# A fused attention and feed-forward kernel: the scores' maximum and bias moved ahead of the probabilities' low halves in VectorE's step

## The chip, the cores and the metric

One core of a Trainium2 chip (trn2). The metric is the device time of one execution of the whole kernel, in microseconds (us). The kernel before has a median of 798.86 us over three runs (798.53, 798.86 and 799.95).

## The reference

The input x is 16 batches of 128 rows by 256. Four blocks follow, each added to x: a first attention over the context with 8 heads of 16, a feed-forward block with ternary weights, a second attention, and a gated ternary feed-forward block. The change is in the second attention only. For it the reference computes, per batch:

```
q = rope(rms_norm(y @ Wq.T))            16 heads of 128,  y = layernorm(x)
k = rope(rms_norm([ctx; y] @ Wk.T))      4 heads of 128,  256 keys
v = [ctx; y] @ Wv.T
probs = softmax(q k.T / sqrt(128))      4 query heads share one key head
x = x + (probs v) @ Wo.T
```

## The kernel before

The second attention is `part_c`. Its work is cut into 64 units: 16 batches times 4 groups, one group being one key head with its four query heads. It is a software pipeline written out by hand: every engine runs a loop over steps s, and in step s each stage works on the unit u = s minus that stage's lag. The lags are PROJ 4 (projections, norm, rope), QK_TURN 5 (a DMA transposes queries and keys), SCORE 6, PROBS 7, LOWS 8 (a DMA transposes the low halves), ATTEND 9, OUT 10. Once per batch, in every fourth step, come HALVES (lag 2), ROWS (lag 1, the layernorm's rows) and LAST (lag 14, the residual). Nothing reorders the work: each engine executes its list in order, and a wait on a semaphore holds everything behind it on that engine.

Precision is kept by splitting float32 values into a float16 high half and a float16 low half. A product takes three passes (high by high, high by low, low by high; `PASSES`), so each stage has an instruction for the high half and one for the low half.

In one step of the steady state the engines do this, in this order (lines of the kernel before):

- **VectorE**: the share of the probabilities, as a scaling (L1321) and a reciprocal (L1324); L1321 waits for ScalarE's four exponentials of the previous step. Then queries times cosine and sine (L1330). Then the low half of the attended rows (L1338). Then `lows(probs, 0)`, two instructions of L1311: the low halves of the probabilities of heads 0 and 1. Once per batch the residual, x_rows (L1345). Then the maximum over the scores of a unit (L1351), which waits for TensorE's scores, and the bias made of it (L1355). Then `lows(probs, 1)`, two more of L1311. Then keys times cosine and sine (two of L1366, which wait for the norm factor r that ScalarE makes at L1301) and the low half of v (L1370). Once per batch the statistics of new rows (L1376, L1380), and a step later their normalised rows (L1385).
- **ScalarE**: the high half of the attended rows (L1245), the high halves of the probabilities (four of L1252, which wait for the share), the sums of squares (four of L1266 after L1330, two of L1272), the high half of v (L1276), a logarithm (L1280), once per batch two small ones (L1286, L1289), then the first exponential (L1235), which waits for the bias, the factor r (L1301) and three more exponentials.
- **TensorE**: the query projection (six matmuls, L1406), the key and value projection (twelve, L1417), the scores (twelve, L1431), the attended rows (six, L1444), the output projection (twelve, L1459). L1417 waits for VectorE's L1370 of the previous step, since there is one bank for keys and values. L1444 waits for L1338. L1459 of a batch's first group waits for the residual L1345 of the batch before it, since there is one bank for the output; by the lags both stand in the same step (s - 10 and s - 14).
- **GpSimd**: the rotation of queries (L1189), their high half (L1193), their low half (L1220, which waits for this step's bias), and the keys' (L1223 to L1228, from L1366 on). The SyncE queue issues the transposes (L1138 for probabilities, L1153 for queries and keys, L1159 for rows).

The stages before and behind overlap with it. The first feed-forward block's last batches share its first steps, the second feed-forward block's first batches its last ones, on the same engines.

The waits that the steps of the prediction use:

```
eng.wait_ge(S["scores"], u + 1)          # VectorE, before L1351
wait(eng, S["v_lo"], u)                  # TensorE, before L1417
if g == 0:
    wait(eng, S["out"], b)               # TensorE, before L1459
eng.wait_ge(S["exps"], u + 1)            # VectorE, before L1321
```

Of the kernel before, what the change touches and what calls it, by code (L numbers as in the profile page):

```python
# [21 lines left out]
ALU = mybir.AluOpType  # L22
# [15 lines left out]
def wait(eng, sem, value):  # L38

    if value > 0:  # L40
        eng.wait_ge(sem, value)
# [847 lines left out]
W_SCALE = 64.0  # L889
# [164 lines left out]
def part_c(core):  # L1054


    c = core
    GROUPS = KV_HEADS
# [8 lines left out]
    LAST = OUT + GROUPS  # L1067
    STEPS = TOTAL + OUT + 1
    P_SCALE = 1024.0
    A_SCALE = 2.0**-10  # L1070
# [34 lines left out]
    A_BANK, O_BANK = c.bank(0), c.bank(1)[:, 0:D]  # L1105
# [10 lines left out]
    S = {n: c.sem("c_" + n) for n in (  # L1116
        "eps", "stats", "rstd", "y", "y_hi", "y_lo", "tables", "q", "kv", "ss_k", "ss_q", "r", "q_cs", "q_rot", "k_cs",
        "k_rot", "v_hi", "v_lo", "q_hi", "q_lo", "k_hi", "k_lo", "scores", "top", "bias", "exps", "share", "p_hi",
        "p_lo", "attn", "a_hi", "a_lo", "o", "out")}
# [5 lines left out]
    def unit(s, lag):  # L1125

        u = s - lag
        return u if 0 <= u < TOTAL else None

    def batch(s, lag):  # L1130


        u = s - lag
        return u // GROUPS if 0 <= u < TOTAL and u % GROUPS == 0 else None
# [172 lines left out]
    def vector(eng):  # L1307
        def lows(u, half):
            eng.wait_ge(S["p_hi"], 2 * u + half + 1)
            for h in range(2 * half, 2 * half + 2):  # L1310
                last = eng.scalar_tensor_tensor(p_hl[:, u % 2, 1, h, :], s_banks(u)[:, h, :],  # L1311
                                                share[:, u % 2, h:h + 1], p_hl[:, u % 2, 0, h, :],
                                                ALU.mult, ALU.subtract)
            last.then_inc(S["p_lo"], 1)

        for s in range(STEPS + 1):
            probs, proj, score, attend = unit(s, PROBS), unit(s, PROJ), unit(s, SCORE), unit(s, OUT)
            if probs is not None:
                u = probs
                eng.wait_ge(S["exps"], u + 1)  # L1320
                eng.tensor_scalar(part[:, u % 2, :], total[:, u % 2, :], 1.0 / P_SCALE, None, ALU.mult)\  # L1321
                   .then_inc(S["share"], 1)
                eng.wait_ge(S["share"], 2 * u + 1)
                eng.reciprocal(share[:, u % 2, :], part[:, u % 2, :]).then_inc(S["share"], 1)  # L1324
            if proj is not None:
                u, b = proj, proj // GROUPS
                eng.wait_ge(S["tables"], b + 1)
                eng.wait_ge(S["q"], u + 1)
                wait(eng, S["q_rot"], u)
                eng.tensor_tensor(  # L1330
                    q_cs[:, :, :, :],
                    Q_BANK.rearrange("p (h d) -> p h d", h=SHARE).unsqueeze(1).broadcast_to([P, 2, SHARE, HEAD_DIM]),
                    turn["q"][:, b % 2, :, :].unsqueeze(2).broadcast_to([P, 2, SHARE, HEAD_DIM]), ALU.mult)\
                   .then_inc(S["q_cs"], 1)
            if attend is not None:
                u = attend
                eng.wait_ge(S["a_hi"], u + 1)
                eng.scalar_tensor_tensor(a_t[:, u % 2, 1, :], A_BANK, A_SCALE, a_t[:, u % 2, 0, :], ALU.mult,  # L1338
                                         ALU.subtract).then_inc(S["a_lo"], 1)
            if probs is not None:  # L1340
                lows(probs, 0)
            b = batch(s, LAST)
            if b is not None:
                eng.wait_ge(S["o"], GROUPS * (b + 1))
                eng.scalar_tensor_tensor(c.x_rows[:, b, :], O_BANK, 1.0 / (W_SCALE * W_SCALE * P_SCALE * A_SCALE),  # L1345
                                         c.x_rows[:, b, :], ALU.mult, ALU.add).then_inc(S["out"], 1)
            if score is not None:
                u = score
                eng.wait_ge(S["scores"], u + 1)
                wait(eng, S["bias"], u - 1)  # L1350
                eng.tensor_reduce(top[:, u % 2, :], s_banks(u), AX.X, ALU.max).then_inc(S["top"], 1)  # L1351
                eng.wait_ge(S["top"], u + 1)
                eng.wait_ge(S["r"], 2 * (u + 1))
                wait(eng, S["exps"], u - 1)
                eng.scalar_tensor_tensor(bias[:, u % 2, :], top[:, u % 2, :], -1.0, r_q(u), ALU.mult, ALU.mult)\  # L1355
                   .then_inc(S["bias"], 1)
            if probs is not None:
                lows(probs, 1)
            if proj is not None:

                u, b = proj, proj // GROUPS
                eng.wait_ge(S["r"], 2 * (u + 1))
                eng.wait_ge(S["v_hi"], u + 1)
                wait(eng, S["k_rot"], u)
                for n in range(2):
                    last = eng.scalar_tensor_tensor(  # L1366
                        k_cs[:, :, n, :], kv_view[:, n, 0, :].unsqueeze(1).broadcast_to([P, 2, HEAD_DIM]), r_k(u, n),
                        turn["k"][:, b % 2, :, n, :], ALU.mult, ALU.mult)
                last.then_inc(S["k_cs"], 1)
                eng.tensor_tensor(v[:, u % V_SLOTS, 1, :, :], kv_view[:, :, 1, :], v[:, u % V_SLOTS, 0, :, :], ALU.subtract)\  # L1370
                   .then_inc(S["v_lo"], 1)
            b = batch(s, 0)
            if b is not None:
                eng.wait_ge(ffn["out"], b + 1)
                wait(eng, S["stats"], 2 * b)
                eng.bn_stats(stats[:, :], c.x_rows[:, b, :]).then_inc(S["stats"], 1)  # L1376
                eng.wait_ge(S["stats"], 2 * b + 1)
                wait(eng, S["y"], b)
                wait(eng, S["rstd"], 2 * b)
                eng.bn_aggr(mv[:, :], stats[:, :]).then_inc(S["stats"], 1)  # L1380
            b = batch(s, ROWS)
            if b is not None:
                eng.wait_ge(S["rstd"], 2 * (b + 1))
                wait(eng, S["y_lo"], b)
                eng.tensor_scalar(y[:, :], c.x_rows[:, b, :], mv[:, 0:1], rstd[:, :], ALU.subtract, ALU.mult)\  # L1385
                   .then_inc(S["y"], 1)
            yield
# [4 lines left out]
    def tensor(eng):  # L1392
        for s in range(STEPS):
# [69 lines left out]
            yield  # L1463

    return sync, pool, scalar, vector, tensor


# [87 lines left out]
```

## Time and profile before

| what | value |
|---|---|
| median of 3 runs | 798.86 us |
| the profiled execution's own time | 800.01 us |
| its span in the trace | 798.3 us |
| granted TensorE clock, mean over the span | 0.961 |
| TensorE matmuls busy | 677.3 us, 85% of the span |
| VectorE busy | 661.1 us, 83% |
| ScalarE busy | 624.3 us, 78% |
| GpSimd busy | 534.5 us, 67% |
| DMA packets | 323795, 99.80 MB |

The second attention takes the larger half of the span: VectorE's first maximum over scores (L1351) starts at 289.4 us and its last at 723.4 us. All four compute engines are in use through it, and in most slices of that stretch TensorE, VectorE and ScalarE each show nine tenths or more.

Engine names in the rows: PE is TensorE's matmul, PEld its weight load, DVE is VectorE, ACT ScalarE, POOL GpSimd, SPq the queue of SyncE. In a timeline a row gives the start in us, the length in us of all the instructions merged into the row, the engine, the line, the operation, what it writes and reads, its shape and how many there are. The bracket at the end is idle time in front of it and who ended it.

### The profile page before, as it was taken

What the parts mean: (1) busy time and instruction counts of PE and PEld (TensorE: products, weight loads), DVE (VectorE), ACT (ScalarE), POOL (GpSimd) and SP (SyncE); (2) the same over time, 40 slices, a digit from 0 to 9 for tenths busy, and PEclk for the clock granted to TensorE, in tenths of its full rate; (3) what the DMA queues carried; (4) which work ended last, traced back from release to release, by engine and by line L of the source; (5) the groups of instructions that cost most, each with busy time, mean ns of one, the idle gap of its engine ahead of it and who ended that gap; (6) DMA issues with size and microseconds to landing.
All of it is one profiled execution on the core that took longest, in us unless ns stands there. A gap on an engine that the chain in (4) does not pass through costs nothing. (4 is left out here: it accounts for less than half of the span.)

```text
span 798.3 us, 17290 instructions
## 1 busy us (share of the span) xinstructions
PE 677.3 (85%) x5139; PEld 423.0 (53%) x5139; DVE 661.1 (83%) x1576; ACT 624.3 (78%) x2122; POOL 534.5 (67%) x764
## 2 busy tenths in 40 slices
PE   0075799999578678999999999999999999978995
PEld 0043255455234345666666666666666666645552
DVE  6756556764689769999999999999999999978994
ACT  0556477777399769999999999999999999968661
POOL 1413756663357888888788878887887888753673
PEclk9997599999799989999999999999999999999997
DMA  8502555542024356897887798788879787865244
GB/s 278 199 1 54 138 155 148 142 129 86 11 67 106 64 106 126 147 144 129 148 139 142 127 154 139 134 138 154 139 135 144 143 136 133 153 113 93 58 125 122
DMA packets 323795, 99.80 MB, mean 125 GB/s; under 512 B 294868, under 2 KB 322934, under 8 KB 323446
## 3 DMA queue, kind: packets, MB, share of 16 engines
q1 hardware_dynamic: 323702, 98.70, 61.7%
q8 instruction: 41, 0.67, 0.4%
q14 instruction: 52, 0.43, 0.2%
HBM read 20.01 MB, written 6.29 MB: 33 GB/s over the span
## 5 line engine op out<-in xcount | busy, mean ns | idle before, releaser
L1235 ACT ACTIVATE psum<-psum,arena 128x256 f32<-128x256 f32 x256 | 135.9, 531 | 21.1 <-DVE arena L1355 21.0
L1311 DVE SCALAR_TENSOR_TENSOR arena<-psum,arena 128x256 f16<-128x256 f32 x256 | 110.9, 474 | 1.1 <-ACT arena L1252 1.1
L1252 ACT ACTIVATE arena<-psum,arena 128x256 f16<-128x256 f32 x256 | 100.3, 474 | 7.4 <-issue 3.4
L1444 PE MATMUL psum<-arena 128*128 128x512 f16 x384 | 94.2, 381 | 8.1 <-DVE arena L1338 7.9
L1189 POOL TENSOR_TENSOR arena<-arena 128x512 f32<-128x512 f32 x64 | 81.1, 1267 | 27.8 <-DVE arena L1330 27.8
L1406 PE MATMUL psum<-wq_t,arena 128*128 128x512 f16 x384 | 94.5, 383 | 5.5 <-ACT arena L1266 2.8
L1431 PE MATMUL psum<-arena 128*128 128x256 f16 x768 | 95.6, 275 | 1.0 <-DMA arena<-arena 0.8
L1459 PE MATMUL psum<-wo_t,arena 128*128 128x256 f16 x768 | 95.0, 274 | 0.1
L305 ACT ACTIVATE arena<-psum 128x1024 f32<-128x1024 f32 x64 | 63.1, 1019 | 33.2 <-PE psum L391 33.2
L1459 PEld LDWEIGHTS psum<-wo_t,arena 128*128 128x128 f16 x768 | 75.5, 98 | 23.2 <-issue 1.1
L1220 POOL TENSOR_TENSOR arena<-arena 128x512 f16<-128x512 f32 x64 | 74.1, 1157 | 20.0 <-DVE arena L1355 19.9
L1431 PEld LDWEIGHTS psum<-arena 128*128 128x128 f16 x768 | 75.3, 99 | 11.4 <-DMA arena<-arena 1.6
L1351 DVE TENSOR_REDUCE arena<-psum 128x4 f32<-128x1024 f32 x64 | 77.8, 1215 | 2.7 <-PE psum L1431 2.4
L1330 DVE TENSOR_TENSOR arena<-psum,arena 128x1024 f32<-128x1024 f32 x64 | 78.4, 1225 | 1.1 <-PE psum L1406 1.1
L1266 ACT ACTIVATE arena<-psum 128x128 f32<-128x128 f32 x256 | 68.2, 304 | 10.6 <-DVE arena L1330 10.6
L1417 PE MATMUL psum<-wkv_t,ctx_t 128*128 128x256 f16 x384 | 54.3, 279 | 13.2 <-DVE arena L1370 12.6
L1366 DVE SCALAR_TENSOR_TENSOR arena<-psum,arena 128x256 f32<-128x256 f32 x128 | 56.1, 480 | 9.3 <-ACT arena L1301 6.7
L1223 POOL TENSOR_TENSOR arena<-arena 128x256 f32<-128x256 f32 x64 | 46.3, 724 | 23.7 <-DVE arena L1366 23.6
L422 PE MATMUL psum<-arena 128*32 128x256 f32 x1024 | 61.9, 383 | 0.0
L1266 ACT ACTIVATION_READ_ACCUMULATOR arena<-psum 128x1 f32 x256 | 60.8, 238 | 0.0
L1444 PEld LDWEIGHTS psum<-arena 128*128 128x128 f16 x384 | 33.7, 97 | 48.0 <-issue 13.6
L1417 PEld LDWEIGHTS psum<-wkv_t,ctx_t 128*128 128x128 f16 x384 | 33.2, 99 | 46.9 <-DVE arena L1370 42.3
(187 smaller groups left out, 1612.5 us busy)
## 6 DMA issues: line engine op xcount, KB each, us to landing
arena<-split_scratch SPq DMA_DIRECT2D x96, 64.0 KB, 2.6
arena<-arena SPq DMA_TRANSPOSE x272, 3.3
split_scratch<-arena SPq DMA_DIRECT2D x32, 128.0 KB, 2.1
arena<-in_L_ffn_w SPq DMA_DIRECT2D x2, 1024.0 KB, 6.8
x_rows<-in_L_xattn_Wq SPq DMA_DIRECT2D x1, 2048.0 KB, 14.4
ctx_t<-in_L_xattn_Wo SPq DMA_DIRECT2D x1, 2048.0 KB, 12.4
x_rows<-in_x SPq DMA_DIRECT2D x16, 128.0 KB, 2.3
arena<-in_ctx SPq DMA_DIRECT2D x16, 128.0 KB, 2.5
```

What stands on the lines that cost most here:

```text
L1189: eng.tensor_tensor(straight(q_rot[:, :, :]), straight(q_cs[:, 0, :, :]), swapped(q_cs[:, 1, :, :]), ALU.add).then_inc(S["q_rot"], 1)
L1235: last = eng.activation(s_banks(u)[:, h, :], s_banks(u)[:, h, :], ACT.Exp, bias=bias[:, u % 2, h:h + 1], scale=r_q(u)[:, h:h + 1], accum_o ...
L1252: hi = eng.activation(p_hl[:, u % 2, 0, h, :], s_banks(u)[:, h, :], ACT.Copy, scale=share[:, u % 2, h:h + 1])
L1266: last = eng.activation(junk[:, h, :], Q_BANK[:, P * h:P * h + P], ACT.Square, accum_out=sums[:, u % 2, h:h + 1])
L1311: last = eng.scalar_tensor_tensor(p_hl[:, u % 2, 1, h, :], s_banks(u)[:, h, :], share[:, u % 2, h:h + 1], p_hl[:, u % 2, 0, h, :], ALU.mul ...
L1330: eng.tensor_tensor(q_cs[:, :, :, :], Q_BANK.rearrange("p (h d) -> p h d", h=SHARE).unsqueeze(1).broadcast_to([P, 2, SHARE, HEAD_DIM]), tu ...
L1351: eng.tensor_reduce(top[:, u % 2, :], s_banks(u), AX.X, ALU.max).then_inc(S["top"], 1)
L1406: mm = eng.matmul(Q_BANK, y_t[:, b % 2, x, k, :], c.wq_t[:, w, k, SHARE * P * g:SHARE * P * g + SHARE * P], start=(n == 0), stop=(n == 5))
L1417: mm = eng.matmul(KV_BANK[:, KEYS * row:KEYS * row + KEYS], x_t, c.wkv_t[:, w, k, g, :, :].rearrange("p a d -> p (a d)"), start=(n == 0), ...
L1431: mm = eng.matmul(s_banks(u)[:, h, :], q_head(u, q, h), k_keys(u, k), start=(n == 0), stop=(n == 2))
L1444: mm = eng.matmul(A_BANK, v[:, u % V_SLOTS, x, k, :], p_t[:, u % 2, w, :, k, :], start=(n == 0), stop=(n == 5))
L1459: mm = eng.matmul(O_BANK, a_t[:, u % 2, a, P * h:P * h + P], c.wo_t[:, w, SHARE * g + h, :], start=(g == 0 and h == 0 and n == 0), stop=(g ...
```

## The change

In VectorE's step the block with the maximum (L1351) and the bias (L1355) is put in front of the first pair of low halves and of the batch's residual. The order was low halves 0 and 1, residual, maximum, bias, low halves 2 and 3. It becomes maximum, bias, low halves 0 and 1, residual, low halves 2 and 3. No instruction is added, removed or altered, and no wait changes; only the order on VectorE does.

```diff
@@ -1337,13 +1337,6 @@
                 eng.wait_ge(S["a_hi"], u + 1)
                 eng.scalar_tensor_tensor(a_t[:, u % 2, 1, :], A_BANK, A_SCALE, a_t[:, u % 2, 0, :], ALU.mult,
                                          ALU.subtract).then_inc(S["a_lo"], 1)
-            if probs is not None:
-                lows(probs, 0)
-            b = batch(s, LAST)
-            if b is not None:
-                eng.wait_ge(S["o"], GROUPS * (b + 1))
-                eng.scalar_tensor_tensor(c.x_rows[:, b, :], O_BANK, 1.0 / (W_SCALE * W_SCALE * P_SCALE * A_SCALE),
-                                         c.x_rows[:, b, :], ALU.mult, ALU.add).then_inc(S["out"], 1)
             if score is not None:
                 u = score
                 eng.wait_ge(S["scores"], u + 1)
@@ -1354,6 +1347,13 @@
                 wait(eng, S["exps"], u - 1)
                 eng.scalar_tensor_tensor(bias[:, u % 2, :], top[:, u % 2, :], -1.0, r_q(u), ALU.mult, ALU.mult)\
                    .then_inc(S["bias"], 1)
+            if probs is not None:
+                lows(probs, 0)
+            b = batch(s, LAST)
+            if b is not None:
+                eng.wait_ge(S["o"], GROUPS * (b + 1))
+                eng.scalar_tensor_tensor(c.x_rows[:, b, :], O_BANK, 1.0 / (W_SCALE * W_SCALE * P_SCALE * A_SCALE),
+                                         c.x_rows[:, b, :], ALU.mult, ALU.add).then_inc(S["out"], 1)
             if probs is not None:
                 lows(probs, 1)
             if proj is not None:
```

## Rows read from the trace of the kernel before

**Rows 1.** Busy time in ten batches of the steady state (us, instructions, clock, DMA share, GB/s)

```profile
407.90:681.30 273.40, 269.02 (x1920) 181.76 (x1919) 259.95 (x560) 260.49 (x1140) 222.88 (x291) 1.00 0.82 141
```

**Rows 2.** Waits of the whole span (us in total, times, longest us)

```profile
ACT psum L1235 <- DVE arena L1355: 21.0, 48, 1.6
...
DVE arena L1321 <- ACT psum L1235: 12.9, 30, 0.4
PE psum L1417 <- DVE arena L1370: 12.6, 20, 1.8
```

**Rows 3.** Timeline of VectorE over one ordinary step

```profile
516.31 0.18 DVE L1355 SCALAR_TENSOR_TENSOR arena<-arena 128x4 f32<-128x4 f32 x1
516.41 0.86 DVE L1311 SCALAR_TENSOR_TENSOR arena<-psum,arena 128x256 f16<-128x256 f32 x2
517.30 0.88 DVE L1366 SCALAR_TENSOR_TENSOR arena<-psum,arena 128x256 f32<-128x256 f32 x2
518.10 0.41 DVE L1370 TENSOR_TENSOR arena<-psum,arena 128x256 f16<-128x256 f32 x1
518.94 0.17 DVE L1321 TENSOR_SCALAR arena<-arena 128x4 f32<-128x4 f32 x1 [0.43 <-ACT psum L1235]
...
520.40 0.68 DVE L1338 SCALAR_TENSOR_TENSOR arena<-psum,arena 128x512 f16<-128x512 f32 x1
521.00 0.87 DVE L1311 SCALAR_TENSOR_TENSOR arena<-psum,arena 128x256 f16<-128x256 f32 x2
521.78 1.22 DVE L1351 TENSOR_REDUCE arena<-psum 128x4 f32<-128x1024 f32 x1
523.03 0.16 DVE L1355 SCALAR_TENSOR_TENSOR arena<-arena 128x4 f32<-128x4 f32 x1
```

**Rows 4.** Timeline of TensorE over the same step

```profile
518.57 0.83 PE L1417 MATMUL psum<-wkv_t,ctx_t 128*128 128x256 f16 x6
...
519.89 1.47 PE L1431 MATMUL psum<-arena 128*128 128x256 f16 x12
...
521.23 1.46 PE L1444 MATMUL psum<-arena 128*128 128x512 f16 x6
```

**Rows 5.** Timeline where a maximum was ready before its scores

```profile
294.26 1.47 PE L1431 MATMUL psum<-arena 128*128 128x256 f16 x12
...
295.77 1.23 DVE L1351 TENSOR_REDUCE arena<-psum 128x4 f32<-128x1024 f32 x1
```

**Rows 6.** Timeline of TensorE over a step in which nothing held it

```profile
661.04 1.46 PE L1406 MATMUL psum<-wq_t,arena 128*128 128x512 f16 x6
662.34 0.82 PE L1417 MATMUL psum<-wkv_t,ctx_t 128*128 128x256 f16 x6
...
663.65 1.47 PE L1431 MATMUL psum<-arena 128*128 128x256 f16 x12
664.96 1.46 PE L1444 MATMUL psum<-arena 128*128 128x512 f16 x6
666.25 1.47 PE L1459 MATMUL psum<-wo_t,arena 128*128 128x256 f16 x12
667.56 1.46 PE L1406 MATMUL psum<-wq_t,arena 128*128 128x512 f16 x6
```

**Rows 7.** Timeline of VectorE in a step with the batch's residual

```profile
672.22 0.41 DVE L1345 SCALAR_TENSOR_TENSOR x_rows<-psum,x_rows 128x256 f32<-128x256 f32 x1
672.55 1.22 DVE L1351 TENSOR_REDUCE arena<-psum 128x4 f32<-128x1024 f32 x1
```

**Rows 8.** The maximum's line from 300 to 700 us: ns min/median/max, first, last start

```profile
L1351 DVE TENSOR_REDUCE arena<-psum x59: 1211/1215/1225, 302.5 to 699.7; 128x4 f32<-128x1024 f32 x59
```

**Rows 9.** Timeline of VectorE in one of the last steps with scores

```profile
714.98 0.66 DVE L1338 SCALAR_TENSOR_TENSOR arena<-psum,arena 128x512 f16<-128x512 f32 x1
716.02 0.88 DVE L1311 SCALAR_TENSOR_TENSOR arena<-psum,arena 128x256 f16<-128x256 f32 x2 [0.38 <-ACT arena L1252]
716.81 1.22 DVE L1351 TENSOR_REDUCE arena<-psum 128x4 f32<-128x1024 f32 x1
```

**Rows 10.** Timeline of TensorE: scores at a lower clock, and projections behind a stall

```profile
286.63 2.77 PE L1431 MATMUL psum<-arena 128*128 128x256 f16 x12
...
313.19 0.83 PE L1417 MATMUL psum<-wkv_t,ctx_t 128*128 128x256 f16 x6 [1.79 <-DVE arena L1370]
```

## The prediction

> **What bounds the kernel now.** I read the busy time of a steady stretch first, then the table of waits, then the timeline of one step on VectorE and TensorE together.
>
> The stretch [rows 1] is ten batches, 40 steps, in 273.4 us: 27.34 us a batch, 6.84 us a step. TensorE is busy 98% of it, VectorE and ScalarE 95% each, so no busy share names the bound. The waits do [rows 2]. ScalarE waits for the bias 48 times (21.0 us), and VectorE waits for the last exponential 30 times (12.9 us). Two engines that wait for each other, step after step, form a loop, and this one sets the pace in many steps. The rest are nearly full on VectorE alone, because of the batch's extra instructions.
>
> The loop of an ordinary step [rows 3]: the bias starts at 516.31. The exponentials let VectorE go on at 518.94, after 0.43 us idle. Share, reciprocal, queries and L1338 take it to 521.00, the first pair of low halves to 521.78, the maximum to the next bias at 523.03. That is 6.72 us, and 0.78 of it (521.00 to 521.78) is the pair that the change takes out. Read this far, the change looks like a gain.
>
> There is a second loop through VectorE [rows 3, 4]. L1370 ends at 518.51 (518.10 + 0.41). TensorE, held by it, starts keys and values at 518.57, scores at 519.89, and these are out before the maximum. From the maximum VectorE runs bias, low halves 2 and 3, keys, and the next L1370. What matters is when the scores are really there. Where VectorE came early [rows 5], the scores started at 294.26 and the maximum at 295.77: 1.51 us later, 0.04 after the end that the trace models. So in the ordinary step the scores were usable at 519.89 + 1.51 = 521.40 and the maximum started at 521.78. It had only 0.38 us to spare.
>
> By the Trainium skill, "Perfetto Trace Analysis", section "Tensor Engine Instruction (MATMUL, LD_WEIGHTS)", a matmul's end is computed, and the acknowledgement of the written bytes and the semaphore follow it; the 0.04 us agrees in sign. Taken as possibly much later, that rule would lengthen the release and raise my sum.
>
> **The change part by part.** All times below count from the start of a step's scores.
>
> Ordinary step. The maximum could now start at 521.00 instead of 521.78, but waits for the scores until 1.51. Then maximum to bias 1.25 (521.78 to 523.03), giving 2.76; bias to low halves 0.10 (516.31 to 516.41), 2.86; first pair 0.78, 3.64; second pair 0.78, 4.42; keys 0.80 (517.30 to 518.10), 5.22; L1370 0.41, 5.63; release of TensorE 0.06, 5.69; keys and values 1.32 (518.57 to 519.89), 7.01 [rows 3 to 5]. The second pair took 0.89 before; I take the 0.78 of the first pair, since the 0.11 was the wait for r, which follows the first exponential and is covered now. The old second loop was 0.78 shorter and had that 0.11: 6.34 us. Its slack of 0.38 is used up and 0.4 more is charged: **the pair leaves a loop of 6.72 and enters one of 6.34, which becomes 7.01**.
>
> Does another engine ask for more? VectorE on its own would reach the maximum 2.38 us behind the start of L1370: 2.90 (518.10 to 521.00) less 0.43 of wait and about 0.1 around it. Scores come 0.41 + 0.06 + 1.32 + 1.51 = 3.30 behind it. So VectorE idles about 0.9 us there. That also hides the statistics or the normalised rows of a batch, both under 0.7. The exponentials release at bias + 2.63 = 5.39, before VectorE wants them at 5.55 (0.33 behind the start of L1370): the old wait goes to nothing. TensorE's own stream is 6.52 us [rows 6], so it idles about half a microsecond a step in front of L1417. L1444 no longer meets L1338's end (521.08 against 521.23 before). GpSimd's queries wait for a bias that comes at the same point, its keys 0.8 later within the longer step, and the transposes keep over a step to land. The queues lose nothing.
>
> Residual step, once per batch. L1345 moves behind the bias and a pair. It starts at 3.64 and ends at 4.05 (0.41 [rows 7]). In this very step TensorE's L1459 opens a new batch's bank and waits for it; queued behind it are the next query projection and the next L1417. Unheld, L1459 would start at 1.31 + 1.29 = 2.60; now 4.05 + 0.06 = 4.11. Then output 1.31, queries 1.30, keys and values 1.31 [rows 6]: next scores at 8.03. VectorE's L1370 ends at 5.96 and is no longer the last. So this step is 8.03, not 7.01: 1.02 more. L1345 itself costs nothing further, under TensorE's stall.
>
> A batch is then 3 x 7.01 + 8.03 = 29.06 us against 27.34.
>
> **Sum.** The first maximum with low halves beside it starts at 295.77 [rows 5], the last of the steady stretch at 699.7 [rows 8]; 59 steps apart, 403.9 us. By the loops: 59 x 7.01 = 413.6, plus 13 residual steps x 1.02 = 13.3, is 426.9: **+23.0 us**. The step after 699.7 already waited elsewhere; I leave it. In two of the last steps with scores the low halves wait 0.38 for their high halves in front of the maximum [rows 9]. Moved, the maximum starts 0.60 (520.40 to 521.00) behind L1338: 715.58 instead of 716.81. ScalarE idled for the bias there (the longest such wait is 1.6 [rows 2]), so I credit 1.2 twice, -2.4. Together +20.5 us. Against the profiled execution (800.0) that is 820.5; the median of the runs is 1.15 lower, so the prediction is 798.86 + 20.5 = **819.4 us**.
>
> Bounds: the release of the maximum rests on one row; 0.05 either way is 3 us over 59 steps. The residual step could lose between 0.8 and 1.3, -3 to +4. The credit at the end lies between 0 and 4. The forecast's own range is 812 to 829.
>
> **The rivals.**
>
> (1) *Faster: the pair was the bound.* If the maximum did not wait for scores, only the first loop would shrink, by 0.78 to 5.94, and TensorE's stream of 6.52 would set the step: 4 x 6.52 = 26.08 a batch, -1.26 for 14.75 batches, -18.6, with the credit -21: 778. For it speaks the table of waits, in which the maximum hardly appears. Against it, the 0.38 us of slack: this needs scores usable by the time VectorE arrives. It decides the other way once they are more than 0.4 late, and the rows say 0.9. Chance 0.07.
>
> (2) *Only the ordinary steps slow down.* If the residual step's stall is absorbed by something the rows don't show, 13.3 falls away: 806. The wait in the code speaks against it. Chance 0.06.
>
> (3) *No difference.* The maximum waits, but what is lost in the second loop is won in the first; this needs a release near 1.3 (the pitch of the scores) and no stall in the residual step. About 799. Chance 0.04.
>
> (4) *The clock falls.* TensorE now stands 1.5 us in front of L1459 once a batch and 0.5 a step. Scores at 1.2 GHz took 2.77 against 1.47 [rows 10]; projection and scores of 13 steps at that level would add about 2.6 each, 34 us: 853. Against it: behind a stall of 1.79 us six matmuls still took 0.83 [rows 10], the 2.4 GHz length, and the stretch of [rows 1] has the clock at 1.00. Chance 0.04. The Trainium skill, "TensorE: Matmul & The Clock Gate", section "What's actually happening", says that idleness throttles the array; by its rule this rival would follow if such stalls count as idle enough.
>
> (5) *ScalarE becomes late as well.* It has about half a microsecond spare a step, and its two extra instructions once a batch use most of it. Up to 0.5 for 15 batches, +7.5 on the forecast, within 812 to 829. Counted with the forecast.
>
> **How the numbers follow.** The forecast with (5) gets 0.77, the others 0.07, 0.06, 0.04 and 0.04; 0.02 is left for causes not named. A range from 806 to 829 takes in the forecast's own and rival (2). It leaves out (1), (3), (4) and the tails. A difference of 0.2% (1.6 us) is about what a measurement of this kernel can tell from none. Faster: 0.08. Same: 0.03. Slower: 0.89.
>
> **What would show it.** Right: in the waits a row of VectorE's L1351 for L1431, near 50 times and 0.7 to 1 us each; L1321 no longer waiting for L1235; TensorE's L1417 held by L1370 in nearly every step with longer stalls; L1459 held by L1345 some 14 times, about 1.5 us each; maxima 7.0 us apart in three steps of four and 8.0 in the fourth. Wrong: steps under 6.84 us, or maxima that start at once while L1444 or L1406 sets the pace; then rival (1). A clock below 0.95 in the steady stretch would be rival (4).

## The result and the profile after

The changed kernel takes 833.88 us (median of five, 832.12 to 835.13) against 798.86: **ratio 1.043, 95% interval 1.041 to 1.044, 35.0 us slower**. The forecast was 819.4, range 806 to 829: the sign was right, the size was not. The profiled execution has a span of 832.1 us against 798.3, so the trace has 33.8 us to account for.

First the waits of the whole span of the changed kernel (us in total, times, longest us). The maximum is now L1344, the bias L1348, the residual L1355; the other lines keep their numbers.

```profile
DVE arena L1344 <- PE psum L1431: 27.0, 61, 1.0
PE psum L1417 <- DVE arena L1370: 26.9, 49, 2.0
...
PE psum L1459 <- DVE x_rows L1355: 24.6, 14, 1.8
...
ACT psum L1235 <- DVE arena L1348: 11.6, 29, 0.9
```

Before, the maximum waited once (2.4 us), the residual held nobody, and VectorE waited 30 times for the last exponential [rows 2]. Now the maximum waits for scores 61 times, L1459 waits for the residual 14 times with 1.76 us each, and the wait for the exponentials is gone. These are the two mechanisms of the forecast. Its signs named a wait of 0.7 to 1 us for the maximum; it is 0.44 on average.

The same on VectorE and TensorE over a step without tables or residual, to be laid beside [rows 3, 4]:

```profile
505.31 1.65 DVE L1311 SCALAR_TENSOR_TENSOR arena<-psum,arena 128x256 f16<-128x256 f32 x4
...
506.88 0.87 DVE L1366 SCALAR_TENSOR_TENSOR arena<-psum,arena 128x256 f32<-128x256 f32 x2
...
507.66 0.41 DVE L1370 TENSOR_TENSOR arena<-psum,arena 128x256 f16<-128x256 f32 x1
...
508.13 0.83 PE L1417 MATMUL psum<-wkv_t,ctx_t 128*128 128x256 f16 x6 [0.30 <-DVE arena L1370]
...
509.45 1.47 PE L1431 MATMUL psum<-arena 128*128 128x256 f16 x12
...
510.96 1.22 DVE L1344 TENSOR_REDUCE arena<-psum 128x4 f32<-128x1024 f32 x1 [0.43 <-PE psum L1431]
...
512.22 0.16 DVE L1348 SCALAR_TENSOR_TENSOR arena<-arena 128x4 f32<-128x4 f32 x1
```

Both pairs of low halves stand together behind the bias (L1311 x4). L1370 ends at 508.07, TensorE's projection starts 0.06 later, the scores at 509.45, the maximum 1.51 behind them. The maximum before this one started at 503.97: 6.99 us, where the forecast had 7.01.

The other two kinds of step are where it went wrong. VectorE and GpSimd beside each other in the step with the normalised rows and in the next, with the residual:

```profile
517.96 1.23 DVE L1344 TENSOR_REDUCE arena<-psum 128x4 f32<-128x1024 f32 x1 [0.32 <-PE psum L1431]
...
519.02 0.72 POOL L1202 TENSOR_TENSOR arena<-trig,norm 128x256 f32<-128x256 f32 x1
519.22 0.54 DVE L1348 SCALAR_TENSOR_TENSOR arena<-arena 128x4 f32<-128x4 f32 x1
...
525.33 1.22 DVE L1344 TENSOR_REDUCE arena<-psum 128x4 f32<-128x1024 f32 x1 [0.22 <-PE psum L1431]
...
526.49 0.72 POOL L1202 TENSOR_TENSOR arena<-trig,norm 128x256 f32<-128x256 f32 x1
526.58 0.65 DVE L1348 SCALAR_TENSOR_TENSOR arena<-arena 128x4 f32<-128x4 f32 x1
...
527.94 0.41 DVE L1355 SCALAR_TENSOR_TENSOR x_rows<-psum,x_rows 128x256 f32<-128x256 f32 x1
...
528.49 1.47 PE L1459 MATMUL psum<-wo_t,arena 128*128 128x256 f16 x12 [1.79 <-DVE x_rows L1355]
...
533.91 1.23 DVE L1344 TENSOR_REDUCE arena<-psum 128x4 f32<-128x1024 f32 x1 [0.74 <-PE psum L1431]
```

The bias is 128 x 4 elements and takes 0.16 us when free. Here it takes 0.54 and 0.65, and both times it ends 0.02 us behind GpSimd's L1202 (519.76 against 519.74; 527.23 against 527.21). The two steps take 7.37 and 8.58 us instead of 7.01 and 8.03. The low halves start 0.46 and 0.57 us behind the start of the bias. A batch is 7.00 + 7.00 + 7.37 + 8.58 = 29.95 us, where the forecast had 29.06.

The bias as a group from 300 to 730 us, first in the changed kernel, then in the kernel before (it is L1348, then L1355; busy us and mean ns before the last bar):

```profile
L1348 DVE SCALAR_TENSOR_TENSOR arena<-arena 128x4 f32<-128x4 f32 x58 | 21.5, 370 | 2.0
```

```profile
L1355 DVE SCALAR_TENSOR_TENSOR arena<-arena 128x4 f32<-128x4 f32 x62 | 10.8, 174 | 2.1
```

The warning stood in the trace of the kernel before, beside the bias of [rows 3] that starts at 516.31:

```profile
515.74 0.73 POOL L1202 TENSOR_TENSOR arena<-trig,norm 128x256 f32<-128x256 f32 x1
```

L1202 ends at 516.47 and that bias at 516.49. 43 of the 64 biases of the kernel before end 0.02 to 0.03 us behind a GpSimd instruction in this way, nearly all with 0.17 to 0.19 us instead of 0.16. There was no room to start it earlier against GpSimd.

**The account.** Between the maxima of steps 7 and 66, 439.58 us passed (295.03 to 734.61); the forecast had 426.9, so 12.7 were missing. 11.2 of them are 13 batches at 29.92 on average instead of 29.06, the other 1.5 lie in the first seven steps, alike in kind: there the bias takes up to 0.65 us, and each step is longer by about what its bias is held. The maximum of step 7 starts 0.7 us earlier, the tail from step 66's maximum to step 69's is 22.83 instead of 23.72 us, and 0.2 us is won behind it: 35.6 - 0.7 - 0.9 - 0.2 = 33.8.

### The profile page after: what moved, and what is told of

Its sections match the earlier page's. It is cut to its first block and busy times, and to the rows that moved or that the text cites. A ratio compares the mean times of both kernels' runs of the same rounds, so it can differ in the third digit from the quotient of the medians.

```text
span 832.1 us, 17290 instructions
## 1 busy us (share of the span) xinstructions
PE 673.1 (81%) x5139; PEld 423.0 (51%) x5139; DVE 680.6 (82%) x1576; ACT 625.5 (75%) x2122; POOL 534.9 (64%) x764
## 5 line engine op out<-in xcount | busy, mean ns | idle before, releaser
L1459 PE MATMUL psum<-wo_t,arena 128*128 128x256 f16 x768 | 95.3, 274 | 24.8 <-DVE x_rows L1355 24.6
L1311 DVE SCALAR_TENSOR_TENSOR arena<-psum,arena 128x256 f16<-128x256 f32 x256 | 106.8, 472 | 0.4 <-ACT arena L1252 0.4
L1459 PEld LDWEIGHTS psum<-wo_t,arena 128*128 128x128 f16 x768 | 74.7, 98 | 51.3 <-issue 32.3
L1344 DVE TENSOR_REDUCE arena<-psum 128x4 f32<-128x1024 f32 x64 | 78.3, 1224 | 27.0 <-PE psum L1431 27.0
L1223 POOL TENSOR_TENSOR arena<-arena 128x256 f32<-128x256 f32 x64 | 46.3, 724 | 60.7 <-DVE arena L1366 60.7
L1330 DVE TENSOR_TENSOR arena<-psum,arena 128x1024 f32<-128x1024 f32 x64 | 78.4, 1224 | 5.7 <-PE psum L1406 5.7
```

Of the source, the lines that this page charges most:

```text
L1330: eng.tensor_tensor(q_cs[:, :, :, :], Q_BANK.rearrange("p (h d) -> p h d", h=SHARE).unsqueeze(1).broadcast_to([P, 2, SHARE, HEAD_DIM]), tu ...
L1459: mm = eng.matmul(O_BANK, a_t[:, u % 2, a, P * h:P * h + P], c.wo_t[:, w, SHARE * g + h, :], start=(g == 0 and h == 0 and n == 0), stop=(g ...
```

## The experiments

Theory L: each step is set by a loop L1370, keys and values, scores, maximum, bias, low halves, keys. Theory R: the residual behind the bias holds L1459, and TensorE's list behind it. Theory G: the bias waits until the GpSimd instruction that is running has ended. Rivals are named with each run. Each ratio is against the kernel before on the same chip. The changed kernel was not run again beside the edits, so a gain over it, given in us, is across chips; on these the kernel before took 798.7 to 800.2 us, and the lengths of the steps in the traces carry the argument.

### The residual put back in front of the maximum

Against the changed kernel, on VectorE:

```diff
+            b = batch(s, LAST)
+            if b is not None:
+                ...
             if score is not None:
                 u = score
                 ...
             if probs is not None:
                 lows(probs, 0)
-            b = batch(s, LAST)
-            if b is not None:
-                ...
             if probs is not None:
                 lows(probs, 1)
```

> The changed kernel with the batch's residual put back ahead of the maximum; the first pair of low halves stays behind the bias. Theory (the residual holds the output projection, TensorE's matmuls queue behind it): the 24.6 us that L1459 waited for the residual vanish, the step with the residual falls from 8.59 us to about 7.5 (the loop through the keys and the maximum, 7.01, plus what the bias loses beside GpSimd's tables, 0.49), so a batch falls from 29.95 to about 28.9 us: 14 batches, -14 to -15 us, about 819 us. Rival (the stall is only a symptom, VectorE's loop through the keys sets every step anyway): under 3 us gained.

Measured: 823.47 us, ratio 1.029 (1.027 to 1.032). That is 10.4 us less than the changed kernel, not 14 to 15. L1459's wait for the residual is gone, which shows theory R, but the batch's steps are 7.00, 7.40, 7.45 and 7.27: 29.12 us where about 28.9 were expected. The bias is now held in three steps of four (0.54, 0.63 and 0.44 us), one more than before, and gives part of the gain back.

### The residual moved alone

Against the kernel before, on VectorE:

```diff
             if probs is not None:
                 lows(probs, 0)
-            b = batch(s, LAST)
-            if b is not None:
-                ...
             if score is not None:
                 u = score
                 ...
+            b = batch(s, LAST)
+            if b is not None:
+                ...
             if probs is not None:
                 lows(probs, 1)
```

> The kernel before with only the residual moved behind the bias; both pairs of low halves stay where they were. Theory: the output projection of a batch's first group starts 1.3 us later, the next scores 0.8 us later, and the next maximum then waits for them, 0.4 us later than before; 14 batches, +5 to +6 us, about 804.5 us, and ordinary steps stay at 6.72 us. Rival (the residual's place does not matter, or VectorE gains its 0.33 us in front of the maximum): 794 to 799 us.

Measured: 802.91 us, ratio 1.0045 (1.0031 to 1.0059), 4 us slower. The residual's half of the change hurts by itself. VectorE and TensorE around it:

```profile
510.55 1.22 DVE L1346 TENSOR_REDUCE arena<-psum 128x4 f32<-128x1024 f32 x1
...
511.89 0.41 DVE L1355 SCALAR_TENSOR_TENSOR x_rows<-psum,x_rows 128x256 f32<-128x256 f32 x1
...
512.45 1.47 PE L1459 MATMUL psum<-wo_t,arena 128*128 128x256 f16 x12 [1.00 <-DVE x_rows L1355]
...
515.31 1.23 DVE L1330 TENSOR_TENSOR arena<-psum,arena 128x1024 f32<-128x1024 f32 x1 [0.23 <-PE psum L1406]
...
517.88 1.23 DVE L1346 TENSOR_REDUCE arena<-psum 128x4 f32<-128x1024 f32 x1
```

The step is 7.33 us, the others 6.71, 6.72 and 6.87, a batch 27.63 against 27.36. The expected +0.4 a batch is +0.27, and what is late is first the query projection (L1330 waits 0.23 for it), which I had overlooked: it is queued behind L1459 too.

### GpSimd's table product moved ahead of the cast

Against the changed kernel, on GpSimd (the product moves, the cast stays):

```diff
+            if s < TOTAL and s % GROUPS:
+                b = s // GROUPS
+                ...
                 eng.wait_ge(S["q_rot"], u + 1)
                 wait(eng, qk_turned[u % 2], 16 * (u // 2))
                 eng.tensor_copy(q_hl(u, 0), flat(q_rot[:, :, :])).then_inc(S["q_hi"], 1)
-            if s < TOTAL and s % GROUPS:
-                b = s // GROUPS
-                ...
```

> The changed kernel with GpSimd's table product (L1202, three steps in four) put directly behind the rotation of the queries instead of behind their high half, so that it ends before the bias starts. Theory (two steps of a batch lose 0.38 and 0.49 us because the bias on VectorE waits until that GpSimd product is over): the bias takes 0.16 to 0.19 us in all steps, the step of 7.37 us falls to 7.0 and the one of 8.59 to 8.1, 14 batches x 0.87 = -12 us, about 822 us. Rival (ScalarE's two extra instructions per batch are what delays these two steps): the steps keep 7.37 and 8.59 us and the time stays within 2 us of 833.9.

Measured: 831.03 us, ratio 1.040 (1.038 to 1.042). Only 2.9 us, not 12, yet not nothing. The trace says why (L1199 is the product now, L1208 the cast):

```profile
516.34 0.73 POOL L1199 TENSOR_TENSOR arena<-trig,norm 128x256 f32<-128x256 f32 x1
517.00 0.61 POOL L1208 CAST arena<-arena 128x512 f16<-128x512 f32 x1
517.21 0.42 DVE L1349 SCALAR_TENSOR_TENSOR arena<-arena 128x4 f32<-128x4 f32 x1
```

The product is out of the way, the cast has slid into its place, and the bias ends 0.02 us behind the cast. It is held by whatever GpSimd instruction is running. The two steps take 7.26 and 8.47.

### Both edits together

Against the changed kernel, on VectorE and on GpSimd:

```diff
+            b = batch(s, LAST)
+            if b is not None:
+                ...
             if score is not None:
                 u = score
                 ...
             if probs is not None:
                 lows(probs, 0)
-            b = batch(s, LAST)
-            if b is not None:
-                ...
 ...
+            if s < TOTAL and s % GROUPS:
+                b = s // GROUPS
+                ...
                 eng.wait_ge(S["q_rot"], u + 1)
                 wait(eng, qk_turned[u % 2], 16 * (u // 2))
                 eng.tensor_copy(q_hl(u, 0), flat(q_rot[:, :, :])).then_inc(S["q_hi"], 1)
-            if s < TOTAL and s % GROUPS:
-                b = s // GROUPS
-                ...
```

> The changed kernel with both edits: the residual ahead of the maximum and the table product behind the rotation. Theory: what is left is the loop through the keys, all steps at 7.01 to 7.1 us, a batch of 28.1 us, so about 14.75 x (29.95 - 28.1) = 27 us under the changed kernel: 807 us, still 8 us above the kernel before. Rival (with both stalls gone the exponentials' loop or TensorE's stream sets the step): steps of 6.5 to 6.8 us, at or below 799 us.

Measured: 817.85 us, ratio 1.023 (1.020 to 1.026), 11 us above the expected 807: steps of 7.00, 7.28, 7.33 and 7.15, with the bias held in three of four by the cast, as in the run before. Neither a step of 6.8 nor one of 7.0 throughout: this edit could not decide.

### GpSimd's batch work moved behind the bias

Against the changed kernel, on GpSimd; the last kept line waits for the bias:

```diff
                 eng.wait_ge(S["q_rot"], u + 1)
                 wait(eng, qk_turned[u % 2], 16 * (u // 2))
                 eng.tensor_copy(q_hl(u, 0), flat(q_rot[:, :, :])).then_inc(S["q_hi"], 1)
-            if s < TOTAL and s % GROUPS:
-                b = s // GROUPS
-                ...
-            b = batch(s, HALVES)
-            if b is not None:
-                ...
 ...
                 eng.tensor_tensor(q_hl(u, 1), flat(q_rot[:, :, :]), q_hl(u, 0), ALU.subtract).then_inc(S["q_lo"], 1)
+            if s < TOTAL and s % GROUPS:
+                b = s // GROUPS
+                ...
+            b = batch(s, HALVES)
+            if b is not None:
+                ...
```

> The changed kernel with GpSimd's table product (L1202) and its two instructions on a batch's rows (L1213, L1215) put behind the queries' low half (L1220), which waits for the bias. So in every step GpSimd has only the queries' high half (a CAST) in front of the bias, and it ends about 0.1 us ahead of it. Theory (the bias reads two SBUF operands and waits until whatever GpSimd instruction is running has ended, a CAST as well as a product): the bias takes 0.16 to 0.19 us in every step, a batch falls from 29.95 by 0.38 + 0.49 to about 29.1 us, 14 batches, -12 us, about 822 us. Rival (only the table product matters, and moving it gives what the earlier move gave, 0.23 us a batch): about 831 us. Rival (ScalarE's extra instructions delay these steps): 833 us, steps of 7.37 and 8.59 us remain.

Measured: 823.03 us, ratio 1.029 (1.027 to 1.031), 10.9 us under the changed kernel where 12 were expected; set against the kernel before on its own chip (800.16), it is 12.2. The step with the normalised rows and the start of the residual step:

```profile
513.24 1.23 DVE L1345 TENSOR_REDUCE arena<-psum 128x4 f32<-128x1024 f32 x1 [0.32 <-PE psum L1432]
513.73 0.61 POOL L1193 CAST arena<-arena 128x512 f16<-128x512 f32 x1
...
514.50 0.16 DVE L1349 SCALAR_TENSOR_TENSOR arena<-arena 128x4 f32<-128x4 f32 x1
...
520.83 0.61 POOL L1193 CAST arena<-arena 128x512 f16<-128x512 f32 x1
...
521.49 0.16 DVE L1349 SCALAR_TENSOR_TENSOR arena<-arena 128x4 f32<-128x4 f32 x1
```

The cast ends at 514.34 and 521.44, before the bias is due, and the bias takes 0.16 us in every step of the steady stretch. The steps are 7.00, 7.00, 7.00 and 8.10, a batch 29.09 us: the forecast's 29.06. This shows theory G, and that ScalarE's extra instructions are not what delayed the two steps.

### The same with the residual in front

Against the changed kernel, on VectorE and on GpSimd:

```diff
+            b = batch(s, LAST)
+            if b is not None:
+                ...
             if score is not None:
                 u = score
                 ...
             if probs is not None:
                 lows(probs, 0)
-            b = batch(s, LAST)
-            if b is not None:
-                ...
 ...
-            if s < TOTAL and s % GROUPS:
-                b = s // GROUPS
-                ...
-            b = batch(s, HALVES)
-            if b is not None:
-                ...
 ...
                 eng.tensor_tensor(q_hl(u, 1), flat(q_rot[:, :, :]), q_hl(u, 0), ALU.subtract).then_inc(S["q_lo"], 1)
+            if s < TOTAL and s % GROUPS:
+                b = s // GROUPS
+                ...
+            b = batch(s, HALVES)
+            if b is not None:
+                ...
```

> The same with the residual ahead of the maximum: both misplaced costs gone, only the first pair of low halves is left behind the bias. Theory: the loop L1370, keys and values, scores, maximum, bias, two pairs, keys sets all four steps at 7.0 us, the residual step at 7.1 to 7.2: a batch of 28.1 to 28.2 us, about 27 us under the changed kernel, 806 to 809 us; still slower than before by 14.75 x 0.8 = 11 us less the 2 us gained at the end. Rival: 799 us or less.

Measured: 813.91 us, ratio 1.018 (1.016 to 1.019), 5 to 8 us above the expectation. Six of the thirteen steady batches are as expected, 7.00, 7.02, 6.98 and 7.00 to 7.08; in these what is left of the loss is theory L alone. In the other seven one step takes 7.5 to 8.1, because the scores wait for a transpose. The waits from 350 to 700 us:

```profile
DVE arena L1350 <- PE psum L1432: 21.2, 37, 1.5
...
PE psum L1432 <- DMA arena<-arena: 4.5, 7, 0.9
```

GpSimd's rows end later, and SyncE, which works in order, issues the next transpose of queries and keys only 1.6 us behind a maximum, in every batch. Where it lands in 3.7 to 3.9 us the scores hardly wait, where it takes 4.4 to 5.0 they do; why it takes longer in seven batches stays open. This is a cost of this edit, not of the change.

### The second pair of low halves behind the keys

Against the changed kernel, on VectorE:

```diff
+            b = batch(s, LAST)
+            if b is not None:
+                ...
             if score is not None:
                 u = score
                 ...
             if probs is not None:
                 lows(probs, 0)
-            b = batch(s, LAST)
-            if b is not None:
-                ...
-            if probs is not None:
-                lows(probs, 1)
             if proj is not None:
                 u, b = proj, proj // GROUPS
                 ...
+            if probs is not None:
+                lows(probs, 1)
```

> Order on VectorE: residual, maximum, bias, low halves 0 and 1, keys and low half of v, low halves 2 and 3. The first pair stays where the change puts it, the second pair leaves the loop through the scores. Theory: that loop falls from 7.01 to 6.2 to 6.3 us, the loop through the exponentials is 5.94, so TensorE's stream (6.52) and ScalarE's work (6.5 to 6.6 with the batch's extras) set the step; a batch of 26.3 to 27.0 us, 782 to 792 us, faster than before. Rival (a step of VectorE is full whatever its order; the change's loss comes from idle time the new order always brings): a batch of 27.4 us or more, 799 us or more.

Measured: 815.39 us, ratio 1.019 (1.017 to 1.020): more than 23 us above the theory's 782 to 792 and in the rival's range of 799 or more. The waits from 350 to 700 us show what became of it:

```profile
DVE arena L1364 <- ACT arena L1301: 16.0, 34, 0.8
...
DVE arena L1349 <- PE psum L1431: 1.5, 3, 0.7
```

The maximum waits for scores three times in 350 us, so the loop through them is released, as theory L says. In its place the keys (L1364) wait for the norm factor r (L1301) from ScalarE. A third loop is the bound: share, high halves, sums of squares, first exponential, r, keys, second pair, share. Steps are 6.80 and 6.81 where VectorE has nothing extra; where rows and statistics stand in them too, they are 7.69 and 7.24. VectorE waits for r in three steps of four (0.33, 0.24 and 0.78 us). In the fourth, the first of 6.80, it waits nowhere, but its bias is held 0.63 us; so theory G has a part in this time too. I had priced two loops and taken the rest for slack.

### The same with GpSimd's batch work behind the bias

Against the run before this one, on GpSimd:

```diff
-            if s < TOTAL and s % GROUPS:
-                b = s // GROUPS
-                ...
-            b = batch(s, HALVES)
-            if b is not None:
-                ...
 ...
                 eng.tensor_tensor(q_hl(u, 1), flat(q_rot[:, :, :]), q_hl(u, 0), ALU.subtract).then_inc(S["q_lo"], 1)
+            if s < TOTAL and s % GROUPS:
+                b = s // GROUPS
+                ...
+            b = batch(s, HALVES)
+            if b is not None:
+                ...
```

> The order of the run before with GpSimd's table product and rows put behind the queries' low half as well. Theory: no bias is held by GpSimd, up to 0.87 us a batch less than with the new order alone where the bias still lies on the pacing loop: 780 to 790 us. Rival (the bias is no longer on the pacing loop): within 2 us of the run with the new order alone.

Measured: 821.43 us, ratio 1.026 (1.023 to 1.028), worse by 6 us than the order alone and outside both expectations. From 350 to 700 us the scores wait 12 times for a transpose, once a batch, 8.9 us in all against 0.6 with the order alone: the same side effect of GpSimd's later work as above, here in every batch (SyncE issues that transpose 1.9 to 2.4 us behind the maximum).

### One low half instead of two

Against the kernel before, on VectorE; `lows` takes a list of heads here and gives its signal with every second head:

```diff
             if probs is not None:
-                lows(probs, 0)
+                lows(probs, (0,))
             b = batch(s, LAST)
             if b is not None:
                 ...
             if score is not None:
                 u = score
                 ...
             if probs is not None:
-                lows(probs, 1)
+                lows(probs, (1, 2, 3))
```

> The kernel before with one low half instead of two moved behind the bias (head 1; head 0 and the residual stay in front of the maximum). Theory of the two loops: the loop through the exponentials falls by 0.39 to 6.33 us, the one through scores and keys rises to 7.01 - 0.39 = 6.62 us, so an ordinary step takes 6.62 us (before 6.72, changed kernel 7.00), and the bias, now as early against GpSimd as in the changed kernel, loses 0.38 and 0.49 us in two steps of a batch: a batch of 27.3 to 27.6 us, 798 to 804 us. Rival (any low half behind the bias costs in proportion): half of the changed kernel's step loss, 6.86 us and 810 us.

Measured: 802.65 us, ratio 1.005 (1.0038 to 1.0063). An unhindered step takes 6.60 us: the expected 6.62 from the loop, below the 6.72 of the kernel before. In three steps of four the maximum starts 1.51 us behind the start of its scores. The others take 7.40, 6.67 and 6.98, with the bias at 0.55 us at the start of the first and the last and at 0.24 in the middle one, a batch of 27.65 us. Time and batch are about as expected. So the cost is no proportion of what is moved: half of the pair makes the free step faster, the whole pair slower. By the two loops the turn lies where they are equally long; no run was made there.

### The same with the table product behind the bias

Against the run before this one, on GpSimd:

```diff
-            if s < TOTAL and s % GROUPS:
-                b = s // GROUPS
-                ...
 ...
                 eng.tensor_tensor(q_hl(u, 1), flat(q_rot[:, :, :]), q_hl(u, 0), ALU.subtract).then_inc(S["q_lo"], 1)
+            if s < TOTAL and s % GROUPS:
+                b = s // GROUPS
+                ...
```

> The same with GpSimd's table product behind the queries' low half, so that it no longer runs when the bias is due. Theory: what the bias lost, 0.5 to 0.87 us a batch, comes back, and ordinary steps stay at 6.62: a batch of 26.7 to 27.0 us, 789 to 795 us, faster than before. Rival (the normalised rows and statistics on VectorE set those steps): no difference to the run before it.

Measured: 797.93 us, ratio 0.9994 (0.9984 to 1.0004): no difference from the kernel before, and 4.7 us better than the run before it. The gain stays short of the 789 to 795 expected: two steps are at 6.60, but the other two at 7.18 and 7.08. In that of 7.08 the bias is still held 0.65 us, now by an instruction on the rows (L1201). That of 7.18 has no held bias; it carries the normalised rows and the residual and takes 7.20 in the kernel before, so there the rival holds.

### The kernel before with the table product behind the bias

Against the kernel before, on GpSimd:

```diff
-            if s < TOTAL and s % GROUPS:
-                b = s // GROUPS
-                ...
 ...
                 eng.tensor_tensor(q_hl(u, 1), flat(q_rot[:, :, :]), q_hl(u, 0), ALU.subtract).then_inc(S["q_lo"], 1)
+            if s < TOTAL and s % GROUPS:
+                b = s // GROUPS
+                ...
```

> The kernel before with only the table product put behind the queries' low half. Theory: in the kernel before the bias comes 0.8 us later against GpSimd than in the changed one and mostly finds it free, so nothing is gained: 797 to 801 us, the bias at 0.16 to 0.19 us in both. Rival (the table product costs the kernel before as much as the changed one): about 787 us.

Measured: 802.84 us, ratio 1.005 (1.0039 to 1.0063). Not a gain of 12 us: in the kernel before this product held nothing up. It is even 4 us slower, outside the expectation, 0.28 us a batch. The trace shows theory G at other places. One step in each batch:

```profile
516.63 0.72 POOL L1215 TENSOR_TENSOR arena<-trig,norm 128x256 f32<-128x256 f32 x1
...
517.32 0.72 POOL L1224 TENSOR_TENSOR arena<-arena 128x256 f32<-128x256 f32 x1
...
517.83 0.24 DVE L1322 TENSOR_SCALAR arena<-arena 128x4 f32<-128x4 f32 x1 [0.43 <-ACT psum L1236]
```

The product, now L1215, puts off the keys' L1224, and the share's scaling (L1322) ends 0.03 us behind that: 0.24 us instead of 0.17, in two steps of four. The normalised rows take 0.81 instead of 0.71, and once a batch the bias takes 0.25 instead of 0.19, behind L1201. Together that is 0.3 us a batch. This place for the product is no remedy.

No version beat the kernel before beyond the measurement.

## Why the prediction was right and wrong

- **The second loop, right.** The ordinary step was forecast at 7.01 and measures 6.99 to 7.00. The step that decides it, a maximum 1.51 us behind the start of its scores, rested on one row [rows 5] and held: it is 1.51 in every steady step of the changed kernel. VectorE idles 0.43 in front of it, not 0.9; another 0.42 went unseen into L1321, which GpSimd's L1223 held (0.58 us for 0.16). The run with one low half gives the same loop at another point (6.62 forecast, 6.60 measured).
- **The residual step, right but for a small term.** The extra of 1.02 over an ordinary step is 1.10 where nothing else disturbs (8.10 against 7.00). L1459 starts 0.14 behind the residual, not 0.06.
- **The failed step: "bias to low halves 0.10", taken from an ordinary step and used for all.** In two steps of four it is 0.46 and 0.57. It failed in the sentence "GpSimd's queries wait for a bias that comes at the same point": I asked what waits for the bias on GpSimd, not what GpSimd is doing when the bias starts. Moving the bias forward put it over the table product. The step with the normalised rows lost 0.37 twelve times and the residual step 0.49 thirteen times, 10.8 us, and the first seven steps lost their 1.5 in the same way: 12.3 of the 12.7 us missing. Removing the holds in the steady stretch gave 10.9 us back (12.2 against the kernel before on the same chip).
- **The credit at the end, too large.** 2.4 us were credited; the steps gained 0.5 and 0.6, and the one before them lost 0.2: 0.9 in all.
- **The range, too narrow.** Its bounds varied terms I had, not a term that was missing. The sum of the forecast, 820.5 in the profiled execution's time, and the 11.2 of the thirteen batches make 831.7; the 1.5 of the credit and 1.5 of the first steps less 0.7 and 0.2 make 833.8 against the profiled execution's 833.9.
- **The rivals.** (1) is refuted: the maximum waits in nearly every step. (2) and (3) fall with the 14 waits of L1459. (4) did not come: the clock is 1.00 over ten batches of the steady stretch, in spite of stalls of 1.8 us. (5) did not either: with GpSimd out of the way the step with the normalised rows takes 7.00, and the residual step 8.10.

## What to carry to other kernels

A step of a software pipeline is the longest of several loops through the engines; an instruction taken out of one loop goes into another, and the slack of that other loop, here 0.38 us against 0.78 moved, is what the forecast of an ordinary step rests on. Count all loops through the engine and ask of each moved wait who is queued behind the one who waits for it. Then lay the new start times against the other engines' instructions: a tiny operation on VectorE can be held by a GpSimd instruction that it shares no data with, and a moved one meets other neighbours.

## What the runs showed of the hardware

A VectorE operation of 128 x 4 elements with two inputs in SBUF (the bias) takes 0.16 us, or ends 0.02 us behind a GpSimd instruction that was running when it started: a TENSOR_TENSOR (0.54 and 0.65 us) or a CAST (0.42 us). The share's scaling, with one input in SBUF, does the same beside L1223:

```profile
507.82 0.72 POOL L1223 TENSOR_TENSOR arena<-arena 128x256 f32<-128x256 f32 x1 [1.13 <-DVE arena L1366]
507.99 0.58 DVE L1321 TENSOR_SCALAR arena<-arena 128x4 f32<-128x4 f32 x1
```

It ends at 508.57, L1223 at 508.54; this one cost nothing, since the maximum behind it waited for scores anyway. Maxima and low halves, which read PSUM, kept their durations beside GpSimd. By the Trainium skill, "SBUF — State Buffer", section "SBUF: two separate sides", VectorE and GpSimd share a port pair that whichever starts first holds for its whole instruction, while the other is blocked; on VectorE's side this concerns operations with two inputs in SBUF, against a GpSimd instruction that reads SBUF, and those in a two-port mode. For the bias the trace agrees, with these numbers. The scaling has one input, and no row shows its mode. The wait appears in no list of waits: it is inside the duration, so the place to see it is a spread between a line's median and maximum duration (for the bias in the kernel before, 177 against 541 ns).

```profile
L1355 DVE SCALAR_TENSOR_TENSOR arena<-arena x64: 161/177/541, 290.7 to 724.7; 128x4 f32<-128x4 f32 x64
```

A whole line can be held in this way and show no spread. The normalised rows (L1385, 128 x 256) have a median of 0.71 us in the kernel before, where each starts while L1223 runs; with the second pair behind the keys, where each starts as a cast ends, the median is 0.40. So the kernel before may lose up to 0.3 us a batch there. No run removes that alone.
